# Moving the negated block choice of VectorE ahead of the experts' key marks

## The reference, cut to what matters

```python
logits_c = jnp.where(c_ok, s_b, NEG)                 # scores of 32 blocks of 16 tokens
_, top_idx = jax.lax.top_k(logits_c, 4)              # the four best blocks of each token and head
...                                                  # attention over the tokens of those blocks
sim = jnp.einsum('btphn,hkpn->pbthk', q, keys)       # 2 x 4 x 64 key scores of the experts
sc, ix = jax.lax.top_k(sim, 8)
all_sc = sx[..., :, None] + sy[..., None, :]
scores, pk = jax.lax.top_k(all_sc, 8)                # the eight best pairs
w = silu(x @ down_embed[idx]) * softmax(scores)
out = ... + silu(x @ Wg + bg) * (x @ Wu + bu) @ Wd + bd
```

## Time and profile before

| | |
|---|---|
| time, median of 3 runs | 1492.09 us (1492.06 to 1493.76) |
| the profiled execution's own time | 1490.08 us |
| its span (first to last instruction) | 1488.3 us |
| mean granted TensorE clock | 0.981 of full |
| busy share PE / PEld / DVE / ACT / POOL | 94 / 70 / 77 / 62 / 64% |
| one step in the middle of the run | 38.39 us |

### The profile page before, as it was taken

The page is one execution under the profiler, slowest core; times in us unless marked ns, Lnnn a source line. Parts: engine busy times, 40 slices in busy tenths (PEclk is TensorE's granted clock), DMA queues, the critical chain, the costliest instruction groups (busy, mean ns, idle before and its releaser), DMA issues. The chain is left out here.

```text
span 1488.3 us, 43616 instructions
## 1 busy us (share of the span) xinstructions
PE 1399.5 (94%) x14864; PEld 1041.1 (70%) x14960; DVE 1148.8 (77%) x4512; ACT 927.1 (62%) x1684; POOL 946.8 (64%) x877
## 2 busy tenths in 40 slices
PE   6899569999999999999999999999999999999978
PEld 4566437777777777777777777777777777777757
DVE  5444378888888888888888888888888888888712
ACT  3776436666666666666666666666666666666641
POOL 4655357777777766666666666666676666666720
PEclk8999969999999999999999999999999999999989
DMA  6556842211112222222212222122222222222027
GB/s 187 202 192 213 269 82 54 52 44 48 46 47 51 52 52 52 52 50 47 47 47 47 50 52 47 48 52 52 52 52 52 52 52 52 66 52 53 9 83 250
DMA packets 217149, 113.76 MB, mean 76 GB/s; under 512 B 128872, under 2 KB 211224, under 8 KB 217112
## 3 DMA queue, kind: packets, MB, share of 16 engines
q1 hardware_dynamic: 216304, 112.88, 27.9%
q10 hardware_dynamic: 808, 0.42, 0.2%
HBM read 73.08 MB, written 40.16 MB: 76 GB/s over the span
## 5 line engine op out<-in xcount | busy, mean ns | idle before, releaser
L1394 DVE TENSOR_REDUCE bmax<-q_bank 128x32 f32<-128x512 f32 (+3 forms) x512 | 221.2, 487 | 34.4 <-PE q_bank L1635 34.2
L1149 POOL TENSOR_TENSOR sumxy<-xy 128x1024 f32<-128x1024 f32 x128 | 246.1, 1942 | 0.0
L1241 ACT ACTIVATE pts<-k_bank 128x512 f32<-128x512 f32 (+2 forms) x384 | 177.4, 490 | 42.2 <-PE k_bank L1670 41.4
L1115 POOL TENSOR_TENSOR pad<-pad 128x1 f32<-128x1 f32 x32 | 6.2, 193 | 287.4 <-DVE top L1413 287.4
L1495 DVE SCALAR_TENSOR_TENSOR mw<-sumxy,c,ex 128x1024 f32<-128x1024 f32 x128 | 162.0, 1287 | 13.4 <-ACT ex L1259 9.6
L1617 PE MATMUL f_bank<-xt,wfu 128*128 128x128 f32 x1024 | 162.4, 281 | 0.0
L1635 PE MATMUL q_bank<-ko,qo 96*128 96x512 bf16 (+3 forms) x512 | 142.6, 306 | 16.9 <-DVE bmax L1394 16.7
L1175 POOL TENSOR_TENSOR cw<-cw,mw 128x1024 f32<-128x1024 f32 x64 | 150.9, 2358 | 11.5 <-ACT mw L1265 8.9
L1617 PE MATMUL f_bank<-xt,wfg 128*128 128x128 f32 x1024 | 150.3, 279 | 0.0
L1617 PEld LDWEIGHTS f_bank<-xt,wfu 128*128 128x128 f32 x1024 | 139.4, 191 | 11.5
L1318 ACT ACTIVATE oT<-k_bank 128x512 f32<-128x512 f32 x64 | 38.2, 597 | 173.8 <-PE k_bank L1685 129.3
(11 more groups left out here) (211 smaller groups left out, 3307.8 us busy)
## 6 DMA issues: line engine op xcount, KB each, us to landing
qo<-s_qs SPq DMA_DIRECT2D x192, 64.0 KB, 2.2
ko<-s_ks SPq DMA_DIRECT2D x186, 64.0 KB, 2.2
s_qs<-parts SPq DMA_DIRECT2D x8, 768.0 KB, 4.7
s_ks<-parts SPq DMA_DIRECT2D x8, 768.0 KB, 6.3
s_v<-vo SPq DMA_DIRECT2D x8, 544.0 KB, 3.0
vv<-s_v SPq DMA_DIRECT2D x32, 136.0 KB, 2.3
vw<-s_v SPq DMA_DIRECT2D x64, 68.0 KB, 2.5
xin<-in_L_attn_x_dram SPq DMA_DIRECT2D x8, 512.0 KB, 7.1
```

Source lines behind the costliest of these rows:

```text
L1149: done("sum_done", g_.tensor_tensor(sumxy[:, h, :, :], xy[:, 0, h, 0:XK, None].broadcast_to([P, XK, KEYS]), xy[:, 1, h, None, :].broadcast ...
L1241: last = s.activation(pts[:, h, OFFS[j]:OFFS[j] + n], bank[:, 0:n], ACT.Exp)
L1394: last = v.tensor_reduce(bmax[:, i, h, 0:n], Q.bank(job)[:, o:o + n * BLK].rearrange("p (n j) -> p n j", j=BLK), AX.X, ALU.max)
```

## The change

The call of `unselected` moves up in VectorE's `step`: from behind the block maxima of head 2 to the place between `expert_sum` and `key_marks`. It computes the same from the same tile. No other engine's list changes, and the first unit (`lead`) keeps its order.

```diff
                     expert_sum(t)
                     if n:
+                        unselected(n, now=t)
                         key_marks(n)
                     gate(t, 1)
                     if n:
                         for part in range(3):
                             block_max(n, 2, part)
                     if n:
-                        unselected(n, now=t)
                         best_pairs(n)
                     up(t, 1)
```

## The result

The changed kernel takes 1510.6 us (median of four runs, 1505.8 to 1511.5) against 1492.6 us before: a ratio of 1.0112, with a 95% interval of 1.0098 to 1.0127. It is 1.1% slower; the forecast was 1510.0 us. The profiled execution was the fastest of the four, with a span of 1504.1 us.

A forecast was written before the change was run, and what follows sets the result against it. VectorE was taken to bound each step up to head 2's first block maximum, PE from there. Removal counted nothing; 30 x 0.58 + 0.47 = 17.9 us gave a profiled 1508.0, plus 2.0 for the median: 1510.0 us, range 1500 to 1516.

The forecast's parts named there:

- a ring of two halves: Main-loop step: PE waits for VectorE up to head 2's first block maximum, then VectorE waits for PE until the result.
- Taken out: Removing the instruction behind head 2's block maxima frees 2.13 us of VectorE per step, costed at no gain.
- The cover: VectorE's idle time behind the old place, 0.73 + 2.05 + 0.89 = 3.7 us, said to hide the removal.
- Put in: Behind `expert_sum`: 0.43 us of instruction plus 0.15 us until its follower starts, 0.58 us per loop step.
- The lower bound of 0.34: Least price of one step in us at the new place, if the link costs nothing.
- The written-out step: The one step outside the loop with a next unit, priced at 0.43 + 0.04 = 0.47 us.
- The near miss with GpSimd: At the new place GpSimd's last sum of weights ends 0.01 us before `unsel` starts, so `unsel` takes 0.43 us.
- The sum: Whole kernel: 30 x 0.58 + 0.47 = 17.9 us slower.
- Signs in the profile: Claimed: VectorE's busy time down 48 us, PE's wait about 0.7 us, step 38.97 us, GpSimd's wait about 2.07 us.
- VectorE counts everywhere: Rival: the step's second half is VectorE-bound too, 48 us faster, 1444 us; chance 0.05.
- absorbed: Rival: PE's slack between head 2's last score job and the result hides the delay, 1492 us; chance 0.06.
- collision: Rival: `unsel` meets GpSimd's sum of weights at the new place; with 0.3 us overlap 27 us, 1519; chance 0.06.

The follow-up runs named there:

- e6: Kernel before, with the second feed-forward gate moved behind the block maxima of head 2: 1488.2 us, ratio 0.9969.
- e5: Changed kernel, with the second feed-forward gate moved behind the block maxima of head 2: 1491.1 us, ratio 0.9998 to the kernel before.
- e10: Changed kernel, with the second gate behind head 2's block maxima and the first up product behind head 1's: 1492.7 us, ratio 1.0003 to the kernel before.
- e8: Kernel before, with the eight best keys behind head 1's block maxima and the second gate behind head 2's: 1488.1 us, ratio 0.9975.
- e9: Kernel before, with the second gate behind head 2's block maxima and the first up product behind head 1's: 1473.5 us, ratio 0.9866.
- e11: Changed kernel, with the moved instruction and its link twice in a row: 1525.2 us, ratio 1.022 to the kernel before.
- e4: Kernel before, with the instruction moved between the best keys and head 1's block maxima, inside GpSimd's last sum of weights: 1579.7 us, ratio 1.0573.
- e7: Kernel before, with the eight best keys moved behind the block maxima of head 1: 1505.7 us, ratio 1.0093.
- e3: Kernel before, with the instruction at its old place replaced by a linked one-column memset in every step: 1492.7 us, ratio 1.0.
- e1: Changed kernel, without VectorE's wait for the end of the moved instruction: 1502.3 us, ratio 1.0073 to the kernel before.
- e2: Changed kernel, with the wait for the best keys and its register instruction ahead of the moved instruction: 1509.6 us, ratio 1.0115 to the kernel before.

## Why the prediction was right

- **The bound.** I read the step as a ring of two halves, with VectorE setting the time up to the first read of head 2 and PE from there. (The row at 636.35 closes the step that I read; the half that leads to 618.59 starts at the result before it, at 597.90.) One number for each ring accounts for all runs: the one through the first read of head 2 takes 38.39 us in the kernel before, the one through the first read of head 1 takes 38.24 (e6). Adding to the former what each edit puts ahead of the read, in us a step, gives +0.58 - 0.60 = -0.02 for e5 and e10 (measured 0.00 and +0.02), -0.60 + 0.48 = -0.12 for e8 (-0.14), -0.60 for e9 (-0.56), +1.05 for e11 (+1.05) and +2.05 for the steps of e4 at full clock (40.44 us, measured 40.44 to 40.53). The 38.24 and the +0.48 are read from e6 and e7, so these two runs do not test them. That PE was 94% busy did not mean that VectorE was free.
- **Taken out: worth nothing.** Shown by e3, and by the wait of 2.10 us at head 3 in the changed kernel. The cover was not quite the one that I named: the waits of 0.73, 2.05 and 0.89 us, 3.7 in all, hardly shrank (0.73, 2.08 and 0.89 in e3). A new wait ahead of them, at the first job of head 3, took the time; PE fills that bank no sooner.
- **Put in: 0.58 us.** Measured 0.58 in the steps of the loop, with each part seen by itself: 0.43 + 0.15 in the changed profile, 0.34 without the link (e1), 0.47 with the register instruction ahead (e2). The lower bound of 0.34 was thus the price of a kernel that could have been written. The written-out step was mis-sized: 0.47 forecast, 0.73 measured, of which 0.27 are the longer stop of PE ahead of L1766. The term rests on no row of that step behind the bank read; why PE stops there stays open.
- **The near miss with GpSimd.** `unsel` took 0.42 to 0.43 us in all 32 cases, so the sum of weights was over in time, but by nothing: from the third unit on, `unsel` starts within 0.02 us of the end of that sum in every step of the changed kernel. I had staked the 0.43 on a miss of 0.01 us, and no row told me that it would last; that part of the forecast came true by luck, and 0.06 was a low chance for its rival. The narrow miss is steady, though: in e1, e2 and e5 the two lie within 0.03 us too. e4 shows what it would have cost otherwise, and more than the rival said, since I hadn't counted the clock. For the rule of the Trainium skill, "SBUF — State Buffer", "Who interferes with whom", the trace agrees once more: 1.93 us when issued inside GpSimd's instruction, ending 0.28 us after it.
- **The sum.** 17.9 us forecast, 17.4 by D for 30 of the 31 steps, 18.0 by the medians. The interval of the ratio stands for 14.6 to 19.0 us, so the agreement to 0.1 us is closer than the measurement is; the mechanism is confirmed by the 0.58 us of a step rather than by the sum.
- **Signs in the profile.** All came: 48 us less for VectorE (47.9), PE's weight load waiting 0.7 us (0.72), a step of 38.97 (38.98), GpSimd's wait of 2.07 (2.02).

The rivals fell by e3 (VectorE counts everywhere), by the step's length (absorbed) and by `unsel`'s row (collision). Two things stay open. A step of e7 in the loop costs 0.47 us, while its timeline shows 0.42. And the written-out step cost more than a loop step in most of the slower kernels (0.93 against 0.47 in e7, 1.01 against 0.46 in e2), which no run explains.

## What to carry to other kernels

An instruction that becomes four times shorter can make the kernel slower: ask first on which side of the next bank read it stands, since work ahead of that read is paid in full, as long as the ring through it sets the step (e6), and work behind it is free while the engine waits later on. A linked instruction costs more than its row: add the gap to its follower, and look for register instructions that must be processed in that gap. Before moving covering work away (e7), check what it covers; the move that paid (e9) took elementwise work out from ahead of the bank reads and left the keys there.

## What the runs showed of the hardware that I had not expected

In e4 a stop of PE of 2.3 us in each step was followed in 15 of 29 steps by a stretch at the lower clock level (granted clock 0.75 and 0.82 in the windows above), at a price of 1.2 to 2.9 us for such a step: 41.7 to 43.4 us instead of 40.5. The other 14 steps had the same stop and kept a granted clock of 1.00; what tells the two kinds apart no run here shows. In all other runs PE stopped for VectorE by at most 1.0 us at a time (read from 300 to 1300 us), and the granted clock was 1.00 from 260 to 1380 us. So a long wait of PE can cost more than its own length: in e4 2.9 us a step on average for a collision of 2.1.
